# LoRA-A product in float32 on four 32-column strips, from raw x tiles kept in idle result blocks

## The reference

```python
# layer 0: one weight for all, plus a rank-16 adapter chosen per sequence (8 adapters)
base  = einsum('bsi,oi->bso', x, weight) + bias          # weight 2048 x 2048
low   = einsum('bsi,bri->bsr', x, a_sel)                 # "LoRA-A": 16 rows per adapter
delta = einsum('bsr,bor->bso', low, b_sel)               # "LoRA-B"
x = x + base + scale * delta
# layer 1: one whole 2048 x 2048 weight chosen per sequence out of 16
x = x + einsum('bij,bkj->bik', x, w[adapter_ids])
```

## Time and profile before

| | |
|---|---|
| median of 3 runs | 2740.35 us (2739.03 to 2746.58) |
| profiled execution, its own time | 2741.34 us |
| its span in the trace | 2739.6 us |
| TensorE (PE) busy | 99% |
| VectorE / ScalarE / GpSimd busy | 65% / 50% / 26% |
| DMA | 645 MB, mean 236 GB/s |

### The profile page before, as it was taken

The page is one execution under the profiler, slowest core; times in us unless marked ns, Lnnn a source line. Parts: engine busy times, 40 slices in busy tenths (PEclk is TensorE's granted clock), DMA queues, the critical chain, the costliest instruction groups (busy, mean ns, idle before and its releaser), DMA issues.

```text
span 2739.6 us, 34094 instructions
## 1 busy us (share of the span) xinstructions
PE 2714.4 (99%) x12055; PEld 2248.4 (82%) x12055; DVE 1779.9 (65%) x1595; ACT 1376.3 (50%) x1446; POOL 708.6 (26%) x590
## 2 busy tenths in 40 slices
PE   8899999999999999999999999999999999999999
PEld 6688888888888888888888888888888888888887
DVE  5756776866555557686645565768674656667865
ACT  3333355756443336576644242667663424366665
POOL 4335721312412102141231210114133211112402
PEclk9999999999999999999999999999999999999999
DMA  8758946666845435666784544899997544499996
GB/s 316 291 193 302 348 164 222 217 219 224 307 168 192 150 123 191 209 224 207 235 301 161 185 157 141 297 301 323 313 321 273 175 171 167 148 309 310 316 320 230
DMA packets 198107, 645.17 MB, mean 236 GB/s; under 512 B 23184, under 2 KB 33584, under 8 KB 197936
## 3 DMA queue, kind: packets, MB, share of 16 engines
q1 hardware_dynamic: 197648, 642.46, 68.4%
q10 hardware_dynamic: 288, 0.52, 0.1%
HBM read 651.28 MB, written 58.72 MB: 259 GB/s over the span
## 4 chain that ended last, share of the span: by engine, by line
PE 93%; DMA 3%; POOL 1%; DVE 1%; issue 1%; SPq 0%; ACT 0%; POOLq 0%; DVEq 0%; ACTq 0%
PE acc L878 17%; PE acc L879 17%; PE acc L880 17%; PE acc L825 13%; PE acc L826 13%; PE acc L835 13%; DMA raw<-w 2%; PE acc L796 2%; POOL raw L521 1%; PE acc L847 1%; DMA raw<-xt 1%; DVE ws L759 0%; DMA x_sums<-raw 0%; PE acc L833 0%; DVE raw L694 0%
## 5 line engine op out<-in xcount | busy, mean ns | idle before, releaser
L634 ACT CAST ws<-raw 128x1024 fp32r<-128x1024 f32 (+1 forms) x1104 | 1129.8, 1047 | 1103.8 <-PE acc L835 483.5
L759 DVE TENSOR_TENSOR ws<-raw,ws 128x1024 fp32r<-128x1024 f32 (+2 forms) x1040 | 1329.6, 1303 | 412.4 <-ACT ws L634 408.1
L878 PE MATMUL acc<-ws,ops 128*128 128x512 f32 (+1 forms) x2048 | 796.8, 389 | 0.0
L879 PE MATMUL acc<-ws,ops 128*128 128x512 f32 (+1 forms) x2048 | 796.8, 389 | 0.0
L880 PE MATMUL acc<-ws,ops 128*128 128x512 f32 (+1 forms) x2048 | 796.7, 389 | 0.0
L825 PE MATMUL acc<-ops,ws 128*128 128x512 f32 x1792 | 700.4, 391 | 10.6 <-DVE ws L759 6.8
L826 PE MATMUL acc<-ops,ws 128*128 128x512 f32 x1792 | 699.4, 390 | 0.0
L835 PE MATMUL acc<-ops,ws 128*128 128x512 f32 x1792 | 698.8, 390 | 0.0
L538 POOL TENSOR_TENSOR raw<-raw,eye_s 128x128 f32<-128x128 f32 x384 | 343.4, 924 | 1191.4 <-DMA raw<-w 1191.0
L880 PEld LDWEIGHTS acc<-ws,ops 128*128 128x128 f32 x2048 | 384.5, 188 | 79.8
L878 PEld LDWEIGHTS acc<-ws,ops 128*128 128x128 f32 x2048 | 384.5, 188 | 79.5
(11 more groups left out here) (58 smaller groups left out, 523.6 us busy)
## 6 DMA issues: line engine op xcount, KB each, us to landing
raw<-w SPq DMA_DIRECT2D x928, 512.0 KB
raw<-xt SPq DMA_DIRECT2D x172, 512.0 KB
raw<-w_sums SPq DMA_DIRECT2D x104, 512.0 KB
out<-ost SPq DMA_DIRECT2D x128, 256.0 KB, 6.6
w_sums<-raw SPq DMA_DIRECT2D x32, 512.0 KB, 5.4
x_sums<-raw SPq DMA_DIRECT2D x16, 512.0 KB, 3.9
raw<-x_sums SPq DMA_DIRECT2D x16, 512.0 KB
raw<-a SPq DMA_DIRECT2D x80, 64.0 KB
```

Source lines behind the costliest of these rows:

```text
L634: ins = eng.copy(hi, src)
L759: ins = eng.tensor_tensor(lo, src, hi, ALU.subtract)
L878: eng.matmul(acc, yh, wh, start=begin, stop=False)
L879: eng.matmul(acc, yh, wl, start=False, stop=False)
```

## The change

LoRA-A is no longer done with split operands. `a0` is stored in HBM with 32 columns per t (16 of the adapter, 16 zero, left or right by the parity of the sequence). Each LA block is 8 (t) x 4 (b) matmuls in plain float32, a stationary of 32 columns and a moving operand of 128 columns, sequence b on column strip b of the array (`tile_position=(0, 32 * b)`), each writing the 32 x 128 corner of its own. The moving operand is the raw x tile, which therefore stays on chip: in `cb[:, 1..3]`, idle at that time. The `a0` tiles stay in the output buffers `ost`. LA blocks now stand at (k = 0, after o = 6: i = 0 and 2) and (before k = 2: i = 1 and 3). Their casts, subtracts, and GpSimd sign and add go. Sums of x take the tiles in `cb` as an operand, so b11 and b12 aren't loaded again for k = 1, nor b21 for k = 3; b22 is loaded a second time. The x tiles of the next quad are loaded in the second half of layer 1. The mask is three VectorE instructions instead of sixteen, at planned time 26 instead of 50. LoRA-B uses 96 rows instead of 128.

```diff
 def plan_blocks():
-            if k in (2, 5):
-                blocks.append(("LA", g, 1 if k == 2 else 3))
+            if k == 2:
+                blocks += [("LA", g, 1), ("LA", g, 3)]
             for o in range(HT):
                 blocks.append(("W", g, k, o))
+                if (k, o) == (0, LA_AT):                      # LA_AT = 6
+                    blocks += [("LA", g, 0), ("LA", g, 2)]
-            if k in (0, 4):
-                blocks.append(("LA", g, 0 if k == 0 else 2))
...
-        return [[b11], [b12, b22, b11], [b21], [("t2", g, b), b21], [b12, b22], [b22], [b11, b12]][k]
+        return [[], [b22], [], [("t2", g, b)], [b12, b22], [b22], [b11, b12]][k]
...
+    extra = [(-41.0, ("first",))]
+    for g in range(NG):
+        la_key = 14.0
+        if g:
+            la_key = te[at["S", g - 1, 1, C1 - 1, NU - 1, 2]] + 8.0
+            begin = ts[at["S", g - 1, 1, 0, 0, 0]]
+            extra += [(begin + 20.0 + 8.0 * b + 32.0 * n, ("x", g, i, b, 0)) for n, i in enumerate((1, 3, 2))
+                      for b in range(G)]
+        else:
+            extra += [(splits_key["X", 0, i % 2 + 1, b] - 0.1, ("x", 0, i, b, 0)) for i in (2, 3) for b in range(G)]
+        extra.append((la_key, ("la", g, 0)))
+        extra.append((te[at["LA", g, 2]] + 0.6, ("la", g, 1)))
+        extra += [(te[at["W", g, 1, 2]] + 4.0 * b, ("x", g, 1, b, 1)) for b in range(G)]
...
+        def acca_of(h, b):
+            return (bank[3] if h else acca)[32 * b:32 * b + 32, P * b:P * b + P]
...
         def _(eng):   # SyncE
+                if what[0] == "la":
+                    if j:
+                        eng.wait_ge(s_mm, at["LA", g, 2] + 1)
+                    elif g:
+                        while stored < g * len(stores) // NG:
+                            store(*stores[stored][1:])
+                            stored += 1
+                        for i in range(NOST):
+                            eng.wait_ge(s_out[i], 16 * (g * NB * C1 // NOST // NG))
+                    for h in range(2):
+                        for b in range(G):
+                            src = a0[bass.ds(order(2 * g + h, 2)[b], 1), b % 2, j].rearrange("a p n -> (a p) n")
+                            cols = slice(256 * (b % 2), 256 * (b % 2) + 256)
+                            eng.dma_start(ost[:, 2 * h + b // 2, cols], src).then_inc(s_la[h], 16)
...
         def _(eng):   # VectorE, mask
+                    eng.tensor_tensor(pick, idsb_f.unsqueeze(2).to_broadcast([P, NB, NA]),
+                                      scal_s[:, NA:2 * NA].unsqueeze(1).to_broadcast([P, NB, NA]), ALU.is_equal)
+                    eng.tensor_tensor(pick, pick, scal_s[:, 0:NA].unsqueeze(1).to_broadcast([P, NB, NA]), ALU.mult)
+                    eng.tensor_reduce(mask[:], pick, mybir.AxisListType.X, ALU.add).then_inc(s_mask, 1)
...
         def _(eng):   # TensorE
                     for t in range(HT):
-                        for w in range(2):
-                            ins = eng.matmul(acca[:], a_view(n)[:, t, :], ops[:, h + t, w, :], ...)
+                        for b in range(G):
+                            ins = eng.matmul(acca_of(h, b), la(h, b, t), xt_tile(c, b)[:, P * t:P * t + P],
+                                             start=(ih == 0 and t == 0), stop=(ih == 1 and t == HT - 1),
+                                             tile_position=(0, 32 * b))
```

More of the change, by code:

```diff
@@ L90, in raws_of @@
                 [("w0", o + HT, 0), ("w0", o + HT, 1)]][k]
-    if kind == "XH":
-        return [("x", 0, 0, index[1], 0)] if index[0] == 0 else []
     if kind == "X":
         g, k, b = index
[L95 to L99, removed]
+        b11, _, b12, b22 = (("x", g, h, b, i) for h in range(2) for i in range(2))
+        return [[],
+                [b22],
+                [],
+                [("t2", g, b)],
                 [b12, b22],
@@ L130, in pool_steps @@
     if kind == "X":
-        return {1: ["sub", "add"], 3: ["sub"], 4: ["sub"], 6: ["sub"]}.get(index[1], [])
-    if kind == "LA":
-        return {2: ["neg"], 3: ["add"]}.get(index[1], [])
+        return {1: ["minus", "plus"], 3: ["less"], 4: ["sub"], 6: ["sub"]}.get(index[1], [])
     if kind == "S":
@@ L137, in pool_steps, with program @@
     return []
-def program(nc, xt, a0, w0, w1, bt, bias, ids, half, scal, eye, out):
+def program(nc, xt, a0, w0, w1, bt, bias, ids, scal, eye, out):
     blocks = plan_blocks()
@@ L148, in program @@
         te.append(now)
-    slots = [b for b in blocks if b[0] in ("W", "LA", "S")]
+    slots = [b for b in blocks if b[0] in ("W", "S")]
     bs_done = ["LB", "LB"]
@@ L212, in program @@
     splits.sort()
+    splits_key = {(kind, *index): key for key, _, kind, index in splits}
     number = {(kind, *index): n for n, (_, _, kind, index) in enumerate(splits)}
@@ L219, in x_split @@
         return max(number["X", g, k, b] for b in range(G))
-    place, prior, landed, raws = [], [], [], {}
+    place, prior, landed, raws, ring = [], [], [], {}, 0
     owner = [None] * NRAW
@@ L225, in program @@
     pool_no, pool_total = {}, 0
-    for n, (_, _, kind, index) in enumerate(splits):
+    extra = [(-41.0, ("first",))]
[11 more added lines that the diff above has]
+        extra += [(te[at["W", g, 1, 2]] + 4.0 * b, ("x", g, 1, b, 1)) for b in range(G)]
+    extra.sort()
+    split_of = {}
+    for n, (key_, _, kind, index) in enumerate(splits):
+        while extra and extra[0][0] <= key_:
+            split_of[len(place)] = (-1, 0, extra.pop(0)[1])
+            place.append(None)
+            prior.append(None)
+            landed.append(0)
         raws[n] = []
@@ L330, in raw_tile @@
                 return t[0:2 * RANK]
[L331 removed]
+            return t
         def cube(g, h, u):
```

219 lines of the change are left out of this document (122 added, 97 removed).

## The result

| | before | changed kernel |
|---|---|---|
| median | 2740.47 us (2739.03 to 2746.58, 4 runs) | 2758.94 us (2753.09 to 2759.44, 4 runs) |
| profiled execution / its span | 2741.34 / 2739.6 us | 2758.53 / 2756.4 us |
| mean granted clock | 0.999 | 0.992 |

The changed kernel is slower by 0.6%: ratio 1.0058, 95% interval 1.0038 to 1.0079. I had forecast 2721, between 2703 and 2749.

What follows compares the result with a forecast made beforehand. TensorE was taken to bound quads 1 to 3, DMA quad 0. LA blocks -22.9, quad 0 0 and boundaries +3 made -19.9 us: from 2741.3 to 2721.4, said as 2721 for the median, range 2703 to 2749.

Steps and rivals of the forecast that it cites:

- LA blocks: TensorE's 16 LoRA-A blocks: 2.2 us each instead of 3.63, 22.9 us gained.
- (a): Rival on LA blocks: strips overlap by two only, 3.6 us per block, 3.8 with switches; 2742 us, chance 0.22.
- (b): Rival on LA blocks: strips run one after another, 7.3 us per block; about 2803 us, chance 0.07.
- The boundary: Between quads, three times: SP waits for stores before loading; 1 us of stall each, 3 in all, ends 0 and 7.
- Quad 0: First quad: a 3 us stall in k = 1, less stall later; net 0, between 8 less and 8 more.
- my signs: Trace signs that would show the forecast right, among them quad 1 starting near 701 us.
- k = 5: In quad 0: less LA work as cover for loads through a full DMA; 2 us lost.
- Mask: VectorE's mask in quad 0: three instructions taking 0.6 to 2 us instead of 5.9, and earlier.
- The sum: All terms: -22.9 for LA blocks, 0 for quad 0, +3 for boundaries, -19.9 us in total.
- The second wait: SP's wait for LA(g, 2), 42.6 us into quads 1 to 3: covered by 2 us, so no stall.
- The moved x tiles: Twelve x tiles loaded in layer 1's second half: cost taken as 0, above 5 us.
- Rival (c): Strips as forecast, but SP's waits cost 5 to 8 us at each boundary and in quad 0; 2741 us, chance 0.07.

Runs made afterwards that it cites:

- e7: Changed kernel with a0 loads issued by ScalarE instead of SP, and splits of x sums for k = 1 planned 4 us later in quads 1 to 3: 2709.15 us.
- e6: Changed kernel with all 64 float32 products of an LA pair on one column strip instead of four: 2841.49 us.
- e2: Changed kernel with the second eight a0 loads planned 16 us after LA(g, 2) instead of 0.6 us: 2741.36 us.
- e4: Kernel before with only the mask changed, four short instructions at planned time 26 instead of sixteen at 50: 2738.22 us.
- e1: Changed kernel with the first eight a0 loads of quads 1 to 3 planned 20 us after the quad's start instead of 8: 2743.73 us.

## Why the prediction was wrong

**What bounds the kernel: right.** TensorE's work counts nearly one for one in quads 1 to 3: e7's are 6.6 us shorter than before, for 7.25 us less LA work.

**LA blocks: the term was mis-sized, to the good.** I took 2.2 us a block, of which 0.24 for weight loads and 0.16 for the switches. The blocks themselves take 1.81, four strips streaming at once: a pair is 3.63 us from its start to the start of the next W block, 16 x 0.227, with nothing for weight loads. The switches do cost something, by the starts of the matmuls (e7; it is the same at all 8 pairs of the changed kernel, and before the steps stay at 0.227 at every LA block that waits for nothing):

```profile
787.39 0.39 PE L912 MATMUL acc<-ops,ws 128*128 128x512 f32 x1
787.71 3.70 PE L873 MATMUL acc<-cb,ost 128*32 128x128 f32 x128
791.34 0.50 PE L902 MATMUL acc<-ops,ws 128*128 128x512 f32 x1
791.67 0.40 PE L903 MATMUL acc<-ops,ws 128*128 128x512 f32 x1
```

The step into the strips is 0.32 us and the first one out of them 0.33, instead of 0.227; with the next few, 0.23 us are lost for each pair, where I had put 2 x 0.16. The rule of the Trainium skill, "TensorEngine Tiling (Array Packing)", "Key Properties", that changing the mode drains the array, agrees in that a switch costs time. So a block costs 1.93 us, and 16 of them gain 27 us where I had 22.9. That is 0.45 of the 0.7 us by which e7's quads exceed 675.6 - 7.25; the other 0.2 us are LoRA-B's matmuls, which now start 119 ns apart instead of 113. The 3.9 times for four strips (e6) stand against the 3.2 that I scaled from the Trainium skill, "TensorE: Matmul & The Clock Gate", section on the measured speedup; the measurement decides. Rivals (a) and (b) fall with it: a record of one strip takes 14.1/128 = 0.110 us, as (a) said, but four strips' records take 0.028, so the second matmul of one product doesn't hold up the next strip.

**The boundary: the step that failed.** It said that behind SP's wait stand "only tiles that are needed 5.4 us apart and take 1.5 to load, so it doesn't grow", and took 1 us. For W(g, 0, 3) that was too little already: 1.63, 2.91 and 4.13 us in the three quads, 8.7 where I had 3. And b22 for X(g, 1, 1) stands behind the wait too, and its two sums on GpSimd stand in front of W(g, 0, 4)'s cast on ScalarE, since that engine is in order. GpSimd and ScalarE after:

```profile
726.06 5.94 POOL L579 TENSOR_TENSOR raw<-raw,cb 128x1024 f32<-128x1024 f32 x2 [1.12 <-DMA raw<-xt]
```
```profile
732.03 1.05 ACT L698 CAST ops<-raw 128x1024 fp32r<-128x1024 f32 x1 [5.52 <-POOL raw L579]
732.98 1.04 ACT L698 CAST ws<-raw 128x1024 fp32r<-128x1024 f32 x1
```

Behind it VectorE, by its timeline and the chain (up to TensorE's start at 739.55):

```profile
733.11 3.11 DVE L820 TENSOR_TENSOR ops<-raw,ops 128x1024 fp32r<-128x1024 f32 x1 [5.83 <-ACT ops L698]
...
736.22 3.29 DVE ws L820
```

The weight was there; its cast came only at 732.98, behind that of the x tile, and VectorE's two subtracts then took over 3 us each instead of 1.2 beside GpSimd's next sums. 6.49 us of stall came of it (4.89 and 1.21 in the next quads), and of that the slow clock. In all the boundaries cost 38.0 us where the sum had 3: 8.7 at W(g, 0, 3), 12.6 at W(g, 0, 4), 2.1 at the second wait, 10.8 of slow clock and 3.9 of other losses. I had asked what SP's queue holds behind the wait, and followed only one kind of it through the engines.

**Quad 0: right in place, wrong in size.** I had SP stand still until 59.9 (59.5 measured) and W(0, 1, 1) ready at 73.7, a stall of 3 us. It was ready at 79.5, and the stall was 9.1. GpSimd's and VectorE's rows:

```profile
73.56 2.34 POOL L589 TENSOR_TENSOR raw<-raw 128x1024 f32<-128x1024 f32 x1 [19.61 <-DMA raw<-w]
78.27 1.22 DVE L820 TENSOR_TENSOR ws<-raw,ws 128x1024 fp32r<-128x1024 f32 x1 [1.11 <-ACT ws L698]
```

The tiles asked for from 64.64 on were there at 73.5, and my working has 67.7 for them (73.7 less the four steps behind). SP, let go with many free slots, issued six weight tiles, an x tile and two saves within 6 us, and the chain shows 8.3 us for one of them ("65.12 8.32 DMA raw<-w" is its row). I take the reason to be that all of them share the DMA engines (share 0.99 from 70 to 80 us); no run separates that. And I let both kernels be "paced by DMA" from there, as if SP's wait cost no more than the one stall. But the DMA share is 0.01 for 10 us in a part of the kernel that is bound by DMA, and that is lost for good: k = 2 began at 133.1 us where I had 125, and e2 got 12.2 us back by LA(0, 1). Quad 0 was to gain 5.7 us (703.2; the 701 of my signs forgot the 2 us of k = 5) and lost 0.4.

**Mask: 5.6 us, not 0.6 to 2.** Two of its instructions took 2.6 and 2.5 us beside GpSimd's work. The stall behind the old mask goes, as I said. By itself the change of the mask is worth 3 us by the medians and 5 by the profiled executions (e4), and k = 1 gives none of it back.

**The sum.** From -19.9 to +16.7 are 36.6 us: +35.0 at the boundaries and +7.7 in quad 0, less 6.1 by which the LA blocks were better (29.0 for 22.9; their switches are in the other two). With both waits gone and the order mended (e7) the same strips and mask give 31 us.

**The second wait in later quads** I called covered by 2 us; it cost 0.8, 1.0 and 0.3. **The moved x tiles** cost nothing, as forecast: no stall from 1800 to 2070 us, with 358 GB/s from 1900 to 2055. **k = 5** lost nothing: 1.5 us of stall where 1.9 stood. **Rival (c)** named the mechanism, SP's waits, at "5 to 8 us at each boundary", and had 0.07; they were 10 to 15 with the clock.

## What to carry to other kernels

An in-order DMA queue that runs ahead of the engines turns any wait for the engines into lost prefetch: the wait is not as long as the event is late, but as long as the queue was ahead of it (24 us here, up to 762.9, for `a0` tiles that nobody read before 813). Put such a load late in the order, or better on a queue that runs just in time. And when a queue restarts, follow every kind of tile behind the wait through each in-order engine, since a weight can be there and still stand behind another tile's sum.

## What the runs showed of the hardware

- Four float32 products on four column strips take 0.227 us together, 0.028 us per matmul record, with a weight load for each; on one strip they take 3.9 times that.
- Going into the strips and out of them costs TensorE 0.23 us for each pair of LA blocks, at all 8 places.
- In the changed kernel, after 4.1 to 9.1 us without a matmul the first one lasted 0.79 us, and matmuls went on at 1.2 GHz for a time (clock 0.71 from 740 to 750 us); after 0.3 to 2.9 us it lasted 0.50. Between lie 3.4 us with 0.79 and 3.6 with 0.50, both in e1. A short first matmul doesn't mean that the clock stays: behind the gap of 2.91 us before 1410.4 the granted clock fell to 0.50 from 1411.3 to 1414.7.
- A VectorE instruction beside a GpSimd sum can last far longer: a 1.23 us subtract takes 3.1 to 3.4 (733.11 above), and a 256-element instruction of the mask 2.6, where the next one like it, with GpSimd idle, takes 0.43 (e4). No run varied this alone.
